# A causal convolution as 64 products of 128 x 128 instead of 256 of 128 x 32, with x loaded by channel quarter and time

## What is computed

```python
x = x + conv(x, cond)          # per channel, causal along time, 32 taps: w = cond[:, None, :]
ada = (cond @ ada_w + ada_b)   # shift1, scale1, gate1, shift2, scale2, gate2
x1 = ln(x) * (1 + scale1) + shift1
q, k, v = split(x1 @ qkv_w + qkv_b)          # 16 heads of 128
x = x + gate1 * (softmax(q k^T / sqrt(128)) v @ out_w + out_b)
x2 = ln(x) * (1 + scale2) + shift2
x = x + gate2 * (gelu(x2 @ ffn_w1 + ffn_b1) @ ffn_w2 + ffn_b2)
```

## Time and profile before

| | |
|---|---|
| median of 3 runs | 334.75 us (332.64 to 336.67) |
| the profiled execution | 332.91 us |
| its span in the trace | 331.1 us |
| PE busy | 305.3 us, 92% of the span |
| DVE, ACT, POOL busy | 151.1, 155.2, 80.6 us (46%, 47%, 24%) |
| chain that ended last | PE 84%, DVE 8%, issue 3%, DMA 2% of the span |
| bytes by DMA | 15.74 MB |

### The profile page before, as it was taken

The page is one execution under the profiler, slowest core; times in us unless marked ns, Lnnn a source line. Parts: engine busy times, 40 slices in busy tenths (PEclk is TensorE's granted clock), DMA queues, the critical chain, the costliest instruction groups (busy, mean ns, idle before and its releaser), DMA issues.

```text
span 331.1 us, 7543 instructions
## 1 busy us (share of the span) xinstructions
PE 305.3 (92%) x3279; PEld 258.3 (78%) x3279; DVE 151.1 (46%) x237; ACT 155.2 (47%) x259; POOL 80.6 (24%) x70
## 2 busy tenths in 40 slices
PE   0854989999999999999999999999999999999994
PEld 0854879788888888888888888888888787688884
DVE  4612283366324326327224432432534799773232
ACT  3333323555266444536525526634543647742910
POOL 8200077120063020034103006302003345420400
PEclk9999998999999999999999999999999999999998
DMA  6780023010023002004202001400100000000011
GB/s 204 194 317 6 4 79 113 4 65 0 2 65 107 21 2 63 2 0 129 63 0 63 0 0 63 128 2 2 63 2 1 2 2 0 0 2 0 0 65 63
DMA packets 10056, 15.74 MB, mean 48 GB/s; under 512 B 837, under 2 KB 6061, under 8 KB 9901
## 3 DMA queue, kind: packets, MB, share of 16 engines
q1 hardware_dynamic: 9712, 15.24, 14.6%
q10 hardware_dynamic: 317, 0.10, 0.1%
HBM read 14.26 MB, written 1.11 MB: 46 GB/s over the span
## 4 chain that ended last, share of the span: by engine, by line
PE 84%; DVE 8%; issue 3%; DMA 2%; ACT 0%; ACTq 0%; POOL 0%
PE bank L986 17%; PE bank L987 17%; PE bank L988 17%; PE bank L1062 8%; PE bank L995 4%; PE bank L996 4%; PE bank L997 4%; PE bank L1048 3%; PE bank L893 2%; PE bank L922 2%; DMA crow<-in_cond_dram 2%; PE bank L958 2%; PE bank L908 1%; PE bank L877 1%; DVE yacc L786 1%
## 5 line engine op out<-in xcount | busy, mean ns | idle before, releaser
L308 POOL TENSOR_TENSOR wl<-raw,wh 128x512 fp32r<-128x512 f32 x40 | 52.3, 1331 | 163.5 <-ACT wh L367 163.5
L986 PE MATMUL bank<-x1h,wl 128*128 128x512 f32 (+1 forms) x176 | 67.4, 383 | 1.5 <-DVE x1l L640 1.5
L442 ACT ACTIVATE pool<-bank,bg 128x512 f32<-128x512 f32 x56 | 38.6, 689 | 58.3 <-PE bank L988 58.1
L987 PE MATMUL bank<-x1l,wh 128*128 128x512 f32 (+1 forms) x176 | 65.9, 374 | 0.0
L988 PE MATMUL bank<-x1h,wh 128*128 128x512 f32 (+1 forms) x176 | 65.8, 374 | 0.0
L698 DVE SCALAR_TENSOR_TENSOR ol<-bank,bT,oh 128x512 fp32r<-128x512 f32 x32 | 24.0, 749 | 49.9 <-ACT oh L471 48.9
L986 PEld LDWEIGHTS bank<-x1h,wl 128*128 128x128 f32 x176 | 33.8, 192 | 7.6 <-DVE x1l L640 1.6
L988 PEld LDWEIGHTS bank<-x1h,wh 128*128 128x128 f32 x176 | 33.9, 193 | 5.7
L987 PEld LDWEIGHTS bank<-x1l,wh 128*128 128x128 f32 x176 | 33.9, 193 | 5.6 <-issue 0.2
L1062 PEld LDWEIGHTS bank<-pt,pool 128*128 128x128 f32 x256 | 31.9, 191 | 3.4 <-DVE pt L687 0.8
L1062 PE MATMUL bank<-pt,pool 128*128 128x128 f32 x256 | 32.8, 276 | 0.6 <-DVE ol L698 0.4
(11 more groups left out here) (110 smaller groups left out, 429.3 us busy)
## 6 DMA issues: line engine op xcount, KB each, us to landing
raw<-in_L_cond_qkv_w_dram SPq DMA_DIRECT2D x12, 512.0 KB, 3.9
raw<-in_L_cond_out_w_dram SPq DMA_DIRECT2D x4, 512.0 KB, 3.6
raw<-in_L_cond_ffn_w_dram SPq DMA_DIRECT2D x4, 512.0 KB, 3.4
pool<-in_x_dram SPq DMA_DIRECT2D x2, 512.0 KB, 4.2
pool<-cond_padded SPq DMA_DIRECT2D x4, 256.0 KB, 4.7
adaw<-in_L_cond_ada_w_dram SPq DMA_DIRECT2D x1, 1024.0 KB, 7.7
out_dram<-pool SPq DMA_DIRECT2D x4, 256.0 KB, 2.2
adaw<-in_L_cond_ada_w_dram SPq DMA_DIRECT2D x1, 512.0 KB, 6.3
```

The lines of the kernel that those rows point to most:

```text
L308: g.tensor_tensor(wl[:, cols], raw[:, cols], wh[:, cols].bitcast(F32), ALU.subtract)\
L442: a.activation(dst, src, ACT.Identity, bias=bg[:, j // GH, j % GH:j % GH + 1])\
L986: pe.matmul(dst, wl[:, w_cols], a_hi, start=start, stop=False)
L987: pe.matmul(dst, wh[:, w_cols], a_lo, start=False, stop=False)
```

## The change

The triangles are now placed block-diagonally and x is not: `toep` is [128, 64 slots, 4 quarters, 32], zero but for the block of each quarter, and sixteen copies (DVE two quarters, ACT and POOL one each, for each of four slot groups) fill it from `toep_in` (`BLOCKS_DVE`, `BLOCKS_ACT`, `BLOCKS_POOL`, semaphores `s_tp`). x is loaded by four DMAs, two on SP's queue and two on ACT's, so that partition 32 g + t holds time t of quarter g for all batches; the runs in DRAM are 64 channels, 256 bytes. `conv(k)` is 16 products of a 128 x 128 stationary side with 32 columns, 64 in all. The 16 transposes of x are gone; four products of `pick` with 512 columns of `xq` put x into the banks `CB[k]` ahead, and the convolution is added to it there, so that `turn` no longer adds.

The order changes too. The padded conditions go ahead of everything on SP's queue, and their four reads ahead of `adaw` and the biases; the first weights go ahead of the rest of `adaw`. The `modulation` is cut into four parts of 4, 4, 8 and 8 products (`ADA_PARTS`); the first comes after `conv(3)`, the third after the first projections. `mean(0)` comes ahead of `turn(1)`, and `turn(3)` is moved behind the first three `project_chunk` banks. Pieces 0 to 3 of the first low parts are made by POOL ahead of `rstd(0)`, pieces 4 and 5 by DVE (`s_vlow`).

The core of the diff:

```diff
-        xtok = pool[:, 6144:8192].rearrange("p (n c) -> p n c", c=C)
-        toep = pool[:, 0:2048].rearrange("p (s u) -> p s u", u=T)
+        xq = pool[:, 0:2048].rearrange("p (b s) -> p b s", b=B)
...
-        ADA_PARTS = [(0, ADA1), (ADA1, 2 * ADA1), (2 * ADA1, ADA)]
+        ADA_PARTS = [(CT, 2 * CT), (0, CT), (ADA1, 2 * ADA1), (2 * ADA1, ADA)]
...
+            sp.dma_start(pad_rows(0, T), cond.rearrange("k (g s) -> k g s", g=QB)).then_inc(s_pad, 16)
+            for g in (0, 1):
+                sp.dma_start(xq[T * g:T * (g + 1), :, :], x_v[:, :, SLOTS * g:SLOTS * (g + 1)]).then_inc(s_x, 16)
             sp.wait_ge(s_pad, 32)
...
+            g.wait_ge(s_tp[NX - 1], QB)
+            low_parts(0, range(0, 4))
             rstd(0)
-            low_parts(0, range(0, 4))
+            g.wait_ge(s_vlow, 2)
+            g.wait_ge(s_wlo, 4)
+            g.sem_inc(s_wlo, 2)
             rstd(1)
-            low_parts(0, range(4, 6))
...
+                pe.matmul(CB[k][:, :], pick[:, :, :, :].rearrange("p k a u -> p (k a u)"),
+                          xq[:, :, CBLK * k:CBLK * (k + 1)].rearrange("p b s -> p s b"),
+                          start=True, stop=False, skip_group_check=True)
...
                 for s in range(CBLK):
                     c = CBLK * k + s
-                    for j in range(QB):
-                        m = pe.matmul(CB[k][T * j:T * (j + 1), B * s:B * (s + 1)], toep[:, c, :],
-                                      xq[:, j, c, :, :].rearrange("p i n -> p (i n)"), start=True, stop=True)
+                    m = pe.matmul(CB[k][:, B * s:B * (s + 1)], toep[:, c, :, :].rearrange("p j u -> p (j u)"),
+                                  xq[:, :, c], start=False, stop=(s == CBLK - 1), skip_group_check=True)
...
+            conv(0)
+            conv(1)
+            pe.wait_ge(s_row[1], 16 * 5)
+            pe.transpose(XB[0][:, 0:NBIAS], rows[:, :], ident[0:NBIAS, 0:NBIAS]).then_inc(s_bt, 1)
+            conv(2)
+            conv(3)
             pe.wait_ge(s_adaw[0], 16)
             modulation(0)
-            for k in range(NX):
-                conv(k)
+            pe.wait_ge(s_btc, 1)
             turn(0)
+            mean(0)
             turn(1)
-            mean(0)
-            turn(2)
+            pe.wait_ge(s_adat, ADA_STEPS[0])
+            modulation(1)
             var(0)
             mean(1)
             spread(0)
-            pe.wait_ge(s_adaw[1], 16)
-            modulation(1)
-            turn(3)
+            turn(2)
             var(1)
...
             project_chunk(0, (2,))
-            pe.wait_ge(s_co[1], 2)
+            turn(3)
+            pe.wait_ge(s_adaw[1], 16)
             modulation(2)
             project_chunk(0, (3,))
+            modulation(3)
```

More of the change, by code:

```diff
@@ L110, in cond_resid_block_kernel @@
         vt = sb("vt", [P, TG, T])
-        with nc.sbuf_tensor("x_by_channel", [P, QB, SLOTS, QB, B // QB], F32) as xq:
+        with nc.sbuf_tensor("toep", [P, SLOTS, QB, T], F32) as toep:
             pass
@@ L254, in _ @@
                     .then_inc(s_toep, 16)
+            load_adaw(0, 0, ADA1 * P)
+            for at, src in ((B_QKV, qkv_b), (B_ADA, ada_b), (B_OUT, out_b), (B_F1, ffn_b1), (B_F2, ffn_b2)):
+                n = src.shape[0] // P
+                sp.dma_start(rows[at:at + n, :], src.rearrange("(n p) -> n p", p=P)).then_inc(s_row[1], 16)
+            load_group(0)
             load_adaw(1, ADA1 * P, ADA * P)
-            load_group(0)
             with sp.Fori(1, NG) as hg:
@@ L566, in _ @@
             v.memset(zrows[:, :], 0.0).then_inc(s_zr, 1)
-            for q in (0, 1):
-                v.memset(xq[:, q, :, :, :], 0.0).then_inc(s_xz[0], 1)
+            for k in (0, 1):
+                v.memset(toep[:, CBLK * k:CBLK * (k + 1), :, :], 0.0).then_inc(s_tz[0], 1)
             v.wait_ge(s_condt, 1)
@@ L720, in unit @@
                 softmax_back(hg, u)
-            for n in range(HALVES):
-                v.wait_ge(s_x[n], 16)
-            v.wait_ge(s_xz[0], 2)
-            v.wait_ge(s_xz[1], 2)
-            for i, g in SPREADS_DVE:
-                v.tensor_copy(xq[T * g:T * (g + 1), g, :, i, :],
-                              xtok[T * i:T * (i + 1), :, SLOTS * g:SLOTS * (g + 1)].rearrange("p n s -> p s n"))\
-                    .then_inc(s_xq[1], 1)
-            v.wait_ge(s_toep, 16 * QB)
-            for k in (0, 2):
-                blk = slice(CBLK * k, CBLK * (k + 1))
-                v.tensor_copy(toep[:, blk, :].rearrange("p s u -> p u s"), toep_in[:, :, blk]).then_inc(s_tp[k], 1)
+            v.wait_ge(s_toep, 16 * QB)
+            v.wait_ge(s_tz[0], 2)
+            v.wait_ge(s_tz[1], 2)
+            for k in range(NX):
+                for g in BLOCKS_DVE:
+                    rows_g, slots = slice(T * g, T * (g + 1)), slice(CBLK * k, CBLK * (k + 1))
+                    v.tensor_copy(toep[rows_g, slots, g, :].rearrange("p s u -> p u s"), toep_in[rows_g, :, slots])\
+                        .then_inc(s_tp[k], 1)
+            conv_copy(1)
+            conv_copy(3)
             v.wait_ge(s_btc, 1)
@@ L738, in _ @@
             one_plus(0, SCALE1)
-            conv_copy(1)
-            conv_copy(3)
+            for p in (4, 5):
+                cols = slice(PIECE * p, PIECE * (p + 1))
+                v.wait_ge(s_whi, p + 1)
+                v.tensor_tensor(wl[:, cols], raw[:, cols], wh[:, cols].bitcast(F32), ALU.subtract).then_inc(s_vlow, 1)
+            centre(0)
             xc_copy(1)
-            centre(0)
+            modulation(1)
             scale_up(0)
```

127 lines of the change are left out of this document (54 added, 73 removed).

## The result

The changed kernel takes 348.9 us (median of 4 runs, 347.88 to 350.47) where the kernel before takes 333.69 (4 runs, 332.16 to 336.67): 1.045 times as long, interval 1.036 to 1.054. The forecast was 345 with a range of 335 to 352. The profiled execution took 349.56 us, its span is 347.7 against 331.1, 16.6 more.

The account below looks back on a forecast made before the run. PE is busy nearly throughout from about 48 us, so changes ahead of the first projection move the rest. +7.9 to that projection, +3.0 pushed behind, -0.5 clock: +10.4, 343.3 us profiled, 345 on the median; range 335 to 352.

Parts of the forecast that it names:

- The step that decided: Convolution products: PE's clock falls after about 4 us, 34 records fast, 94 at 222 ns, 24.8 us in all; given 0.70.
- The reading of the earlier trace: Kernel before: PE at its lower level (1.2 GHz) up to about 39 us, though the granted clock reads 1.00.
- The Trainium skill's rule that the prediction weighed: Convolution: sustained back-to-back activity releases the throttle; by it the clock-held rival (332 us, 0.17) would be the forecast.
- The stretch from the end of the convolution to the first projection: Modulation, turn, mean, variance and norm from 41.8 us to the first projection at 56.2.
- Shift and low part at 0.75 us for two: Ahead of the first projection: moving POOL's low parts away ends the slowdown from 2.71 and 1.82, 3.0 us on the chain.
- The start: Start of the convolution products: 17.0 us, bounds 14.5 and 20, nothing gained on 17.24.
- those are cheap: Loads at the start: 4096 packets of 256 B take 2.1 to 6.4 us over 16 engines.
- The rival on the transfers: Start: slow 256 B packets make `crow` late, PE starts at 20 or later, 348 us; 0.05 together with any other.
- the rival of the slow moving side: x products: stepped columns take twice as long, 13.7 instead of 6.9 us, start at 24, 352 us; given 0.08.
- Pushed behind the first projection: Among the projections: turn(3), 1.11 us, and eight modulation products, 1.87 us, now cost +3.0, less 0.5 for the clock.
- 0 to 1.7: Around 50 us: gain in us if PE's time at the lower clock shrinks; 0.5 was taken.
- The last rival: Convolution: reload gaps of PE's list may stay, up to 7 us in the products; given nothing of its own.

Follow-up runs that it names:

- Experiment 2: Changed kernel with 64 moving columns in a run instead of 32 with a step in each convolution product: 335.54 us, ratio 1.002 to the kernel before.
- e_runs: Changed kernel with x read in runs instead of with a step of 64 elements, in x products and convolution: 344.4 us, a single run.
- b_lowfirst: Kernel before with only POOL's low parts 0 to 3 put ahead of rstd(0): 329.31 us, ratio 0.990.
- e_crow: Changed kernel with the load of crow put ahead of the two loads of x on ACT's queue: four runs, 348.75 to 354.62 us.
- e_xruns: Changed kernel with x loaded in runs of 1 KB instead of 256 B, same number of bytes: 344.24 us, ratio 1.035 to the kernel before.
- e_bands: Changed kernel with each 128 x 128 convolution product cut into four of 128 x 32: 338.82 us, ratio 1.016 to the kernel before.
- e_bandruns: e_bands with 32 columns of x read in a run instead of with a step of 64 elements: 340.61 us, ratio 1.023 to the kernel before.
- e_diag: Changed kernel with compact triangles, four copies, no zeros, and products of 32 x 32 by 32 columns: 338.04 us, ratio 1.016 to the kernel before.

## Why the prediction was right

**Right by its mechanism.** The step that decided was the clock, and it held: 24.96 us for the convolution against 24.8 in the sum, full clock at first, then half, 215 ns a record. Experiment 2 shows the cause, by doubling the columns, with e_runs to show that reading them in a run isn't what did it. How long the clock stays up is less certain than the one trace looks: the first 64 records took 8.42 to 12.15 us in six traces, so that 24.96 so near to 24.8 is in part luck. The reading of the earlier trace rows, that PE stood at half clock where the granted clock says 1.00, is borne out by the window of b_lowfirst. The Trainium skill's rule that the prediction weighed ("TensorE: Matmul & The Clock Gate", Part 1, sustained activity releases the throttle) does not hold for this stream, which was busy in 20.00 of 20 us at half clock, and does for the same loads with 64 columns. The stretch from the end of the convolution to the first projection was put at 14.4 and took 14.46. Shift and low part at 0.75 us for two were right, and their place on the chain is shown by b_lowfirst, at 1.6 us for the pair and 1.5 for the clock.

**The start was sized too small.** 17.0 was forecast, 20.01 came, just at the bound of 20. The failed step is "those are cheap": the small packets were priced by their share of the engines' time, 2.1 to 6.4 us spread over all 16, and `crow` was put at 10. It landed at 12.5, and x with it (e_crow); in runs of 1 KB both are 2.8 us earlier (e_xruns). The triangles were late as well, their first group placed at about 18.8 us and not at 16.2. The rival on the transfers named this, with PE starting "at 20 or later" and 348 us, and was given less than 0.05. Two smaller misses hid behind it: DVE places a block in 7.99/8 = 1.0 us and not 0.62, beside POOL at the same work, and the x records never fell from 0.86 to 0.43 us, since they read with a step (e_runs). That was the rival of the slow moving side, in small: priced at 7 us with the x products at 13.7 and given 0.08, it cost 0.85 us, with the x products at 7.23.

**Pushed behind the first projection.** +3.0 less 0.5 = 2.5 was forecast; +1.5 came. Of the 3.07 us of `turn(3)` and modulation products, 1.6 came back, by the fall of the clock at 49 us that is now absent, the upper end of "0 to 1.7" and not 0.5.

**Not foreseen.** The stop in the scores and the clock behind it, +3.9 us. The last rival had the mechanism, but looked for it only in the convolution ("I give this nothing of its own"); it came in the scores 140 us later, where short records had until then met no stop.

Added up on the profiled execution: start 3.0 over, pushed work 1.0 under, the stop 3.9 over, the rest within 0.4; 343.3 was forecast and 349.56 came. That the median was missed by only 3.9 is in part luck: the changed kernel's profile lies 0.7 above its median, the one of before lay 1.8 below the median that the forecast was set on. The range held it with a cost of 3.9 us that no term of the sum has. Two slips change nothing: the three upper bounds add up to +9.6 us, 355 and not 352, and 222 ns against 15 is a fifteenth of the pace, not a tenth.

## What to carry to other kernels

Before merging small products into one with a full stationary side, look at the clock that the merged stream will get, and try it with more moving columns for each weight load: here, with 32 columns for loads of 128, most of the products ran at half clock, with 64 all ran at full, and the second form did twice the work in 58% of the time (14.5 against 24.96 us). A long list of short products is exposed to stops between instructions; if an edit moves the time by some us with no reason at its own place, look for "issue" in the stages far behind, and shift the list to see whether it moves: here by 64 records, half the spacing of the stops, since a whole spacing leaves them where they are. Compare the starts of several traces before one difference is put down to an edit. And test the parts of a change by themselves: the one reordering of GpSimd's work made the kernel 1% faster, inside a change that made it 4.5% slower.

## What the runs showed of the hardware

- The granted clock in the profile reads 1.00 before its first change, also where paces are those of half clock (222 ns in the earlier trace rows; 186 records in 2.74 us read 1.00 in the kernel before and 0.50 in b_lowfirst). Durations of a known form tell the level there.
- A moving operand read with a step of 64 elements cost 30 ns for 32 columns (e_bands), one in runs 9.5 (e_bandruns), both with the full clock granted and with loads of 128 x 32. With loads of 32 x 32 the step gave 15 ns (e_diag). Under 128-column loads at half clock the step cost nothing (13.79 us for 64 records either way).
- PE stopped for 0.9 to 3.9 us within bursts of convolution and score records of 9.5 to 17 ns, and not within the 512 records at 30 ns. In the convolution the bursts begin 127 or 128 records apart. In the changed kernel one such stop cost another 1.6 us by the clock that fell behind it.
- DVE's two-operand operations took 0.75 us for two alone and 1.82 to 2.71 while GpSimd made its low parts.
- Four loads of x in runs of 256 B made transfers on both queues land 2.8 us later than the same bytes in runs of 1 KB, trace against trace; `crow` came 2.0 to 4.9 later over the eight traces.
